# Sums of probabilities issued before the mixed values in four attention stages of a decoder kernel

## The reference, cut to what matters

```
out = einsum('bhij,bhjd->bhid', softmax(scores), v)      # 16 heads
```

## Time and profile before

| what | value |
|---|---|
| median of 3 executions | 4492.57 us |
| lowest and highest of them | 4486.93 and 4498.43 us |
| the profiled execution's own time | 4506.29 us |
| span of its trace (first to last instruction) | 4504.6 us |
| granted TensorE clock, mean over the span | 0.942 of 2.4 GHz |

### The profile page before, as it was taken

The page is one execution under the profiler, slowest core; times in us unless marked ns, Lnnn a source line. Parts: engine busy times, 40 slices in busy tenths (PEclk is TensorE's granted clock), DMA queues, the critical chain, the costliest instruction groups (busy, mean ns, idle before and its releaser), DMA issues. The chain is left out here.

```text
span 4504.6 us, 97054 instructions
## 1 busy us (share of the span) xinstructions
PE 3952.7 (88%) x39200; PEld 2466.0 (55%) x39200; DVE 2364.7 (52%) x5435; ACT 1537.6 (34%) x3480; POOL 880.3 (20%) x1516
## 2 busy tenths in 40 slices
PE   6998898898799879889889987988987998798898
PEld 4884344465588434446558733444655883344565
DVE  5774534553677453455367644345436764533553
ACT  4542222431454222243145422224314542222431
POOL 2430101130243010112024301011202430101220
PEclk9999899989999999999989998999898999899999
DMA  2001000000000100000000010000000001000000
GB/s 84 3 3 59 11 10 19 23 37 26 27 3 3 59 20 5 14 24 37 29 25 3 13 49 20 3 16 24 37 27 27 3 13 49 20 18 1 24 37 29
DMA packets 11005, 105.10 MB, mean 23 GB/s; under 512 B 1148, under 2 KB 5552, under 8 KB 6192
## 3 DMA queue, kind: packets, MB, share of 16 engines
q1 hardware_dynamic: 10544, 98.69, 5.7%
HBM read 97.64 MB, written 1.05 MB: 22 GB/s over the span
## 5 line engine op out<-in xcount | busy, mean ns | idle before, releaser
L89 PE MATMUL psum<-ident_bf 128*128 128x512 bf16 x1996 | 541.6, 409 | 150.4 <-DVE l_attn_peak L900 55.3
L89 PEld LDWEIGHTS psum<-ident_bf 128*128 128x128 bf16 x1996 | 196.3, 105 | 405.3 <-issue 154.3
L149 POOL TENSOR_TENSOR norm_rstd<-norm_var,minus_half 128x4 f32<-128x4 f32 x52 | 52.8, 1015 | 1680.7 <-DVE norm_var L160 1607.3
L3259 DVE TENSOR_TENSOR l_attn_xx<-l_attn_xx,psum 128x256 f32<-128x256 f32 x512 | 204.4, 419 | 200.5 <-PE psum L2862 188.6
L3024 ACT ACTIVATE l_attn_ax<-psum 128x128 f32<-128x128 f32 (+1 forms) x768 | 184.6, 279 | 356.3 <-PE psum L2843 241.7
L490 DVE TENSOR_TENSOR l_ffn_hidden<-l_ffn_silu,psum 128x512 f32<-128x512 f32 (+2 forms) x176 | 120.9, 687 | 317.0 <-ACT l_ffn_silu L429 316.8
L429 ACT ACTIVATE l_ffn_silu<-psum 128x512 f32<-128x512 f32 (+1 forms) x208 | 124.1, 597 | 468.8 <-PE psum L398 415.1
L95 PEld LDWEIGHTS psum<-streamed_weights,l_ffn_hidden 128*128 128x128 f32 (+1 forms) x1664 | 215.1, 191 | 114.0 <-issue 99.8
L2858 PE MATMUL psum<-l_attn_ax,l_attn_xx 64*64 64x64 f32 x5120 | 264.5, 222 | 0.0
L2862 PE MATMUL psum<-l_attn_xx,l_attn_ax 64*64 64x64 f32 x5120 | 257.7, 219 | 0.0
L3148 POOL TENSOR_TENSOR l_attn_part<-l_attn_ab,streamed_weights 128x128 f32<-128x128 f32 x640 | 245.4, 414 | 39.4 <-PE psum L2843 20.3
(11 more groups left out here) (531 smaller groups left out, 8115.8 us busy)
## 6 DMA issues: line engine op xcount, KB each, us to landing
streamed_weights<-pack_l_ffn SPq DMA_DIRECT2D x4, 5284.0 KB, 15.3
streamed_weights<-pack_l_ffn SPq DMA_DIRECT2D x4, 3972.0 KB, 11.7
streamed_weights<-pack_l_attn SPq DMA_DIRECT2D x5, 2848.5 KB, 9.5
streamed_weights<-pack_l_xattn SPq DMA_DIRECT2D x4, 2496.0 KB, 8.6
streamed_weights<-pack_l_ffn SPq DMA_DIRECT2D x4, 2192.0 KB, 8.4
streamed_weights<-pack_l_xattn SPq DMA_DIRECT2D x4, 2048.0 KB, 7.9
streamed_weights<-pack_l_ffn SPq DMA_DIRECT2D x4, 1923.0 KB, 8.2
streamed_weights<-pack_l_attn SPq DMA_DIRECT2D x4, 1107.5 KB, 4.9
```

Of the source, the lines that this page charges most:

```text
L89: pe.matmul(self.bank(bank), self.ident_bf[:, :], self.ident_bf[:, :].unsqueeze(1).to_broadcast([P, NT, P]), start=True, stop=True)
L3259: dve.tensor_tensor(both, both, m.psum[:, p, P:384], ALU.subtract).then_inc(x_less, 1)
```

## The change

In the cross attention `mix(g)` issues the four heads' products with the ones first, increments a new semaphore `group_summed` after them, then issues the values' products and increments `group_mixed` as before. VectorE waits for `group_summed` before a reciprocal, and for `group_mixed` before a product.

In the causal attention `products` issues the ones ahead of the values. `group_summed` is incremented once, in the last unit, after its sums. The reciprocal of the second half waits for that; that of the first half still waits for 11 units. Each product waits for `group_mixed` as the reciprocals did.

```diff
@@ cross_attention_stage
+        group_summed = sem("group_summed")
                 def mix(g):
                     pe.wait_ge(exps_ready, g + 1)
-                    for n in range(2):
-                        for r in range(R):
-                            lhsT = v[:, 4 * r + g, :] if n == 0 else m.const["ones_of"][0:S2, g, :]
-                            ins = pe.matmul(m.psum[quad(r), 5 + n, :], lhsT, prob[:, g % 2, r, :], start=g == 0,
-                                            stop=g == G - 1, skip_group_check=True)
+                    for r in range(R):
+                        ins = pe.matmul(m.psum[quad(r), 6, :], m.const["ones_of"][0:S2, g, :], prob[:, g % 2, r, :],
+                                        start=g == 0, stop=g == G - 1, skip_group_check=True)
+                    ins.then_inc(group_summed, 1)
+                    for r in range(R):
+                        ins = pe.matmul(m.psum[quad(r), 5, :], v[:, 4 * r + g, :], prob[:, g % 2, r, :], start=g == 0,
+                                        stop=g == G - 1, skip_group_check=True)
                     ins.then_inc(group_mixed, 1)
...
                 for half in range(2):
                     cols = slice(HALF * half, HALF * half + HALF)
+                    dve.wait_ge(group_summed, G)
+                    dve.reciprocal(inverse[:, cols], m.psum[:, 6, cols]).then_inc(inverse_ready, 1)
                     dve.wait_ge(group_mixed, G)
-                    dve.reciprocal(inverse[:, cols], m.psum[:, 6, cols]).then_inc(inverse_ready, 1)
                     dve.wait_ge(inverse_ready, half + 1)
                     dve.tensor_tensor(mixed[:, cols], m.psum[:, 5, cols], inverse[:, cols], ALU.mult).then_inc(mixed_ready, 1)
@@ causal_attention
+        group_summed = sem("group_summed")
                     def products(u, j, c, lo, hi, bank):
-                        for n in range(2):
+                        for n in (1, 0):
                             for r in range(R):
...
+                            if n == 1 and u == U - 1:
+                                ins.then_inc(group_summed, 1)
                         return ins
...
                 for half in range(2):
                     cols = slice(HALF * half, HALF * half + HALF)
                     bank = far_bank(G - 1) if half else mix_bank(G - 1)
+                    if half:
+                        dve.wait_ge(group_summed, 1)
+                    else:
+                        dve.wait_ge(group_mixed, U - 1)
+                    dve.reciprocal(inverse[:, cols], m.psum[:, bank + 1, cols]).then_inc(inverse_ready, 1)
                     dve.wait_ge(group_mixed, U - 1 + half)
-                    dve.reciprocal(inverse[:, cols], m.psum[:, bank + 1, cols]).then_inc(inverse_ready, 1)
```

## The result

| | median | lowest to highest | executions |
|---|---|---|---|
| before | 4496.18 us | 4486.93 to 4507.93 | 5 |
| after | 4532.68 us | 4521.59 to 4535.68 | 5 |

The recorded ratio is 1.0071, its 95% interval 1.0043 to 1.0099; the medians differ by 36.5 us, a quotient of 1.0081, where 5.6 us less were forecast. The two profiled executions differ by less, 4521.59 - 4506.29 = 15.3 us, since before's is near the top of its executions and after's the lowest of its own.

A forecast was written before the change was run, and what follows sets the result against it. VectorE was taken to end each cross attention by 0.55 us, with TensorE's warm-up next. Eight ends at 0.70 us gave 5.6, causal attentions 0, waits and increments 0: 4492.57 - 5.6 = 4487.0 us, range 4477 to 4498.

The forecast's parts named there:

- Part 1: Cross attention ends: reciprocal starts 0.88 us earlier, TensorE's warm-up then holds the projections; 0.70 us gained each, 5.6 in eight.
- Part 2: Causal attention ends: sums already wait 1.40 and 1.34 us for VectorE, so having them sooner gains 0.
- a sign of being wrong: Causal attentions: the forecast counts as wrong if an end moves by over 0.1 us.
- The slack of 1.4 us: Causal ends: the second half's awaited sums are there 1.40 and 1.34 us before VectorE gets to them.
- Part 3: Added waits on VectorE (32) and increments on TensorE (40): taken as 0; at worst 1.0 us and 0.7 us.
- The estimate by the Trainium skill: TensorE's 40 increments: completions serialize at about 26 ns each, 1.0 us given back at most, gain 4.6 instead of 5.6.
- What disturbs it: Untouched stages: the same code varies with the granted clock, scatter larger than the gain; 0.3%, 13.5 us, tells no change.
- rival B: Later stages: earlier ends shift them against clock falls, 26.3 us more, 4513.3 us; chance 0.04 past the 0.3% bound.
- C: Later stages: the shift against clock falls makes them faster, 36.1 us less, 4450.9 us; chance 0.11 past the bound.
- the last of the signs that I had named: Untouched stages: the forecast is wrong if their clocks differ on the whole by more than the gain.
- Rival A: Cross attention ends don't move: something else ends the stage, or reciprocals beside running products take longer; 4492.6 us, chance 0.06.

The follow-up runs named there:

- before_short: Kernel before, order and semaphores untouched, second half's reciprocal in the cross attentions taking 152 of 256 columns, so ends come earlier (results wrong); ratio to before 1.0064.
- cross_only: Kernel before with the change in the cross attentions alone, causal attentions left as they were; ratio to before 1.0051.
- before_bothwarm: Kernel before with more warm-up products in the causal attentions' turning steps and at the head of two feed-forwards; ratio to before 0.9927, 4464.79 us.
- cross_match: cross_only with 9 warm-up products and one of 192 columns ahead of the second projection, padding its end to the old time; ratio to before 1.0000.
- before_later: Kernel before with 10 instead of 4 warm-up products ahead of the second projection, so cross attention ends come later; ratio to before 1.0013.

## Why the prediction was wrong

- **Part 1, the earlier end: right in size, by luck in part.** 0.72 us an end against 0.70. But I had TensorE's warm-up end the stage, and in fact VectorE still does, by 0.17 us in all eight ends (1.4 us in sum, where the earlier trace rows have 4.4). Two terms were off. The warm-up of 4 is over 3.64 us behind the start of the first 10 (379.55 + 1.03 - 376.94) and not 3.91 (379.52 - 375.61), because the next product starts before the modelled end of a warm-up: the first projection follows at 2.16 us and not 2.33, and the warm-ups behind it at 0.45 and not 0.55. And VectorE's second half is ready for TensorE 5.67 us behind the last group's first products (380.75 - 375.08) and not 5.50 (379.25 - 373.75), of which the two added waits are 0.14. TensorE came 0.27 us sooner and VectorE 0.17 later than I had them, and the later of the two fell where the forecast was.
- **Part 2, the causal attentions: right in that nothing is gained, wrong by 0.15 us an end**, by the added waits. This is past the 0.1 us that I had named as a sign of being wrong. The slack of 1.4 us was read rightly.
- **Part 3, the waits: mis-sized.** I took 0 for a wait that is satisfied while the reciprocal runs, as the queue seemed to run ahead, with 0.03 us as the upper end. It measures 0.07 us in each of the 32 (the gap of 0.10 less 0.03), over twice the bound: 32 x 0.07 = 2.2 us. The increments on TensorE show nothing: the sets of products stay 0.88 us apart with an increment between them. The estimate by the Trainium skill (TensorE: Matmul & The Clock Gate, "The cost: per-tile semaphore tail") stays untested, because that spacing is one of starts and a tail behind the last product wouldn't show in it.
- **"What disturbs it" and rival B: here the forecast failed.** The step was that the terms "carry over to the median", and that a shift of a few microseconds "should redraw and not add". I took the clock's scatter for noise around a mean that the change leaves alone, gave B 0.04 and C 0.11, and set a range of 4477 to 4498 by the scatter of three executions. The sum was 4487.0; the measured 4532.68 is past the range and past B's 4513.3 as well. The runs showed that the scatter is not a fresh draw: the same early end of layer 0's cross attention gives nearly the same length of f0 in every pass (50.1 to 50.4 us, where before has 49.1 to 50.2), and two kernels that share only their timing, before_short and cross_only, have c1 at 128.7 to 128.8 us in all eight passes. With that end alone the whole is 0.73% slower and the granted clock 0.935 instead of 0.944. B had the right sign and the wrong places: its price was c1 and layer 2's feed-forward at their longest, and in the profiles these two changed by +3.9 and -1.1 us, f0, f1 and x2 by +2.7, +4.7 and +4.8. A hint was in the earlier trace rows, lengths of one stage that differ by the clock alone; that they recur is seen only in more passes. And the last of the signs that I had named came true: the untouched stages' clocks differ by more than the gain.
- **Rival A** fell as forecast: reciprocals beside the values' products took 1746 to 1758 ns. **C** had the wrong sign here, though before_bothwarm shows that there are 26.5 us at the medians in that direction.

**Still open:** how the earlier end acts on the stages behind f0, and why it does so again when both waits are filled. The 2.7 us of f0 are a small part of the 36.5, and the profiled executions, 15.3 us apart, don't show where the rest lies. The runs say that it is timing and not the work, that it begins with layer 0's end, and that the clock carries it. I didn't find a rule by which to tell beforehand the ends that cost.

## What to carry to other kernels

Where a trace shows the same stage with two or three lengths at different granted clocks, a local gain of a few microseconds is worth less than where it moves the next fall; price it with the stage's lengths at either clock as outcomes of their own, and with a real chance. To tell a change from its timing, build its twin: the old code made as much shorter, and the new code padded to the old length, checked in the trace to 0.05 us. And filling TensorE's waits ahead of a fall, up to where the awaited data come, is worth its own trial: both fillings gave 0.73% here without the change, the turning steps alone 0.45%, the heads of the feed-forwards alone nothing that can be told.

## What the runs showed of the hardware that I hadn't expected

An added wait on VectorE between a reciprocal and its product, satisfied while the reciprocal runs, costs 0.07 us, though a second instruction can start before the first is over. Stages settle into recurring lengths across passes (c1 near 121.3, 125.7 or 128.7 us in most passes of before, cross_match and before_later), and leaving out work in eight places, 0.65 us each, made a program of 4.5 ms 0.64% slower (4516.22 against 4489.73 us). And TensorE's clock is lost behind waits that look harmless: with 2.1 us of warm-ups, 2.34 us of waiting and then small products it fell in f0 in every pass (49.1 to 50.4 us). Filling that wait kept it up in every pass with the earlier end (48.1 us), but in only one of eight with the old one (49.1 in the others).
